# A macaron transformer layer on one core: three tables of steps written anew, two GpSimd additions held behind VectorE, whole-tile products and three more runs of filling products in the opening

## The reference

```python
def ffn(x):                      # W1: 512x128, W2: 128x512
    Wq1, Wq2 = quantize(W1), quantize(W2)   # clip(round(W / (mean|W| + 1e-5)), -1, 1)
    return relu(x @ Wq1.T + b1) @ Wq2.T + b2
def attn(x):
    q, k, v = (heads(x @ W.T + b) for W, b in ((Wq, bq), (Wk, bk), (Wv, bv)))
    q, k = rope(q, k)
    p = softmax(q @ k.T / sqrt(8))          # 16 heads, 512 x 512 each, for each of 8 sequences
    return merge(p @ v) @ Wo.T + bo
x = x + 0.5 * ffn(layernorm(x))
x = x + attn(layernorm(x))
x = x + 0.5 * ffn(layernorm(x))
```

## Time and profile before

| | |
|---|---|
| median of 3 runs | 520.1 us (518.65 to 523.45) |
| the profiled execution, its own time | 519.27 us |
| its span from the first to the last instruction | 517.5 us |
| TensorE busy / VectorE busy / ScalarE busy / GpSimd busy | 488.3 / 409.2 / 347.5 / 203.5 us |
| mean granted TensorE clock | 0.990 of full speed |
| start of the first `e` of batch 0, 1, 2, 3, 4, 5, 6, 7 | 54.67, 122.00, 180.83, 239.11, 296.37, 348.18, 400.74, 451.62 us |

### The profile page before, as it was taken

The page is one execution under the profiler, slowest core; times in us unless marked ns, Lnnn a source line. Parts: engine busy times, 40 slices in busy tenths (PEclk is TensorE's granted clock), DMA queues, the critical chain, the costliest instruction groups (busy, mean ns, idle before and its releaser), DMA issues.

```text
span 517.5 us, 13169 instructions
## 1 busy us (share of the span) xinstructions
PE 488.3 (94%) x5455; PEld 227.2 (44%) x5455; DVE 409.2 (79%) x644; ACT 347.5 (67%) x429; POOL 203.5 (39%) x226
## 2 busy tenths in 40 slices
PE   6689999899999999999999999999999999998996
PEld 3455435252354535363354533443344334443445
DVE  5776997958998689877897699779987998898124
ACT  5627565757767687577867677766776778578841
POOL 3507065707338080825534183336342650005001
PEclk8998999999999999999999999999999999999999
DMA  8047037203350136203450147024612451000000
GB/s 276 25 163 166 11 120 208 42 4 123 124 125 3 40 125 177 56 3 97 171 125 4 45 146 189 16 63 162 148 23 56 156 149 36 23 3 3 3 22 20
DMA packets 20007, 44.63 MB, mean 86 GB/s; under 512 B 2860, under 2 KB 5420, under 8 KB 18924
## 3 DMA queue, kind: packets, MB, share of 16 engines
q1 hardware_dynamic: 18636, 41.96, 28.4%
q10 hardware_dynamic: 1312, 1.84, 1.0%
HBM read 20.58 MB, written 18.87 MB: 76 GB/s over the span
## 4 chain that ended last, share of the span: by engine, by line
PE 72%; DVE 15%; ACT 6%; issue 3%; DMA 2%; POOL 1%; ACTq 0%; DVEq 0%; POOLq 0%
PE heads_acc L577 19%; PE side L584 18%; PE unit L560 14%; PE unit L541 12%; DVE maxima L906 8%; ACT probs L788 3%; ACT hidden L778 3%; PE side L621 2%; PE side L611 1%; DMA q_scratch<-q_parts 1%; PE heads_acc L652 1%; PE side L606 1%; PE unit L584 1%; DVE stats_ffn L873 1%; DMA resid<-in_x 1%
## 5 line engine op out<-in xcount | busy, mean ns | idle before, releaser
L906 DVE TENSOR_REDUCE maxima<-unit 128x2 f32<-128x1024 f32 x256 | 304.7, 1219 | 57.3 <-PE unit L541 56.4
L788 ACT ACTIVATE probs<-unit 128x1024 f32<-128x1024 f32 x256 | 256.2, 1025 | 99.1 <-PE unit L560 98.2
L577 PE MATMUL heads_acc<-probs,v_heads 128*32 128x512 f32 x1024 | 135.3, 601 | 0.6 <-ACT probs L788 0.4
L560 PE MATMUL unit<-q_stack,k_stack 64*128 64x512 f32 x512 | 118.7, 463 | 5.9 <-DVE maxima L906 5.3
L541 PE MATMUL unit<-k_stack,q_stack 62*128 62x512 f32 x512 | 114.0, 442 | 2.5 <-DVE maxima L906 1.0
L560 PEld LDWEIGHTS unit<-q_stack,k_stack 64*128 64x128 f32 x512 | 47.6, 184 | 72.6 <-DVE maxima L906 33.9
L541 PEld LDWEIGHTS unit<-k_stack,q_stack 62*128 62x128 f32 x512 | 48.3, 185 | 61.9 <-ACT probs L788 30.6
L584 PE MATMUL side<-w_q,hidden 128*32 128x128 f32 x1664 | 53.5, 275 | 0.0
L386 POOL TENSOR_TENSOR rope_a_k<-k,cos_t 128x512 f32<-128x512 f32 x7 | 8.9, 1277 | 101.6 <-ACT k L775 101.6
L584 PEld LDWEIGHTS side<-w_q,hidden 128*32 128x32 f32 x1664 | 43.2, 110 | 12.4 <-issue 8.9
L1062 POOL TENSOR_SCALAR var_eps_ffn<-mean_var_ffn 128x4 f32<-128x4 f32 x15 | 3.7, 249 | 108.1 <-DVE mean_var_ffn L877 108.1
(11 more groups left out here) (144 smaller groups left out, 461.0 us busy)
## 6 DMA issues: line engine op xcount, KB each, us to landing
k_scratch<-k_parts SPq DMA_DIRECT2D x16, 512.0 KB, 2.9
q_scratch<-q_parts SPq DMA_DIRECT2D x14, 512.0 KB, 3.3
k_stack<-k_scratch SPq DMA_DIRECT2D x16, 384.0 KB, 5.4
q_stack<-q_scratch SPq DMA_DIRECT2D x16, 384.0 KB, 6.8
resid<-in_x SPq DMA_DIRECT2D x8, 256.0 KB, 4.8
k_stack<-k_scratch SPq DMA_DIRECT2D x16, 128.0 KB, 2.5
k_swap<-k SPq DMA_DIRECT2D x14, 128.0 KB, 2.3
q_swap<-q SPq DMA_DIRECT2D x14, 128.0 KB, 2.3
```

Source lines behind the costliest of these rows:

```text
L560: mm = pe.matmul(to[:, e, :], k_stack[part, quad // NQ % 2, pair, kt * P:(kt + 1) * P], q_stack[part, quad // NQ % 2, pair, :], start=True ...
L577: mm = pe.matmul(heads_acc[32 * j:32 * j + 32, :], v_heads[:, b % 2, at, ODD * odd:ODD * odd + 32], probs[:, burst % RING, j, :], start=(k ...
L788: act.activation(probs[:, burst % RING, 2 * pp:2 * pp + 2, :], unit_of(PLACE["exp", n]), ACT.Exp, scale=SCALE).then_inc(s_exp, 1)
L906: dve.tensor_reduce(maxima[:, quad % 2, :, r], unit_of(PLACE["max", k]), AX_X, ALU.max).then_inc(s_max, 1)
```

## The change

There are four parts.

1. The strings of `FIRST`, `STEADY` and `LATER` are written anew. Each table keeps its words, so that the same pieces are done; they stand in other places. SP's stores, maxima rows and swaps at the end of a batch now follow the table's order instead of a fixed one.
2. GpSimd waits at two `add_bias`-like additions: `add_bias("ffn1", 1)` in the opening waits until VectorE has written `normed["attn"]` of batch 0, and the last `xb["ffn2"]` waits until VectorE has written all of the last `normed["ffn2"]`.
3. `column_tiles` takes the width as an argument; the steps of `PROLOGUE` use 128 (whole tiles), all others 32 as before. The four `ffn1_down` pieces of batch 2 beside the first `m` are no part of `PROLOGUE` and stay at 32.
4. `fill` runs at three more places: 14 before the wait for the thresholds of the quantisation, 14 before `ffn1_up0` of batch 1, 8 before `ffn1_up0` of batch 2. In `PROLOGUE` a fill now stands ahead of the waits for weights and constants, not behind them.

```diff
 FIRST = [
-    "e m fill1", "e m first_max_T1", "e m m fill2 attn_T@1", "e m m fill2 k@1", "e m m q@1", "e m m ffn1_T@3",
+    "e m fill1", "e first_max_T1 m", "e m m fill2 attn_T@1", "e m m k@1 fill2", "e m m", "e q@1 m m ffn1_T@3",
...
 LATER = [
-    "e m", "e pv m heads_copy1@-1", "e m heads_T1@-1", "e pv m", "e m pv max_T1", "e m out_T", "e m out", "e m pv",
-    "e ffn2_stats m", "e pv m v", "e m", "e pv max_T2 m", "e m ffn2_T", "e m pv", "e m ffn2_up0",
+    "e m", "e pv m heads_copy1@-1", "e m pv", "e max_T1 m", "e m heads_T1@-1", "e m pv", "e m out_T", "e m out", "e m pv",
+    "e ffn2_stats m", "e pv pv m", "e v m", "e m pv max_T2", "e m ffn2_T", "e m pv ffn2_up0", "e m attn_stats ffn2_up1",
...
-FILL = {("ffn1_up", 0, 0): 8, ("k_first", 0, 0): 6}
+FILL = {("ffn1_up", 0, 0): 8, ("ffn1_up", 0, 1): 14, ("ffn1_up", 0, 2): 8, ("k_first", 0, 0): 6}
+FILL_BEFORE_THR = 14
...
-                if 0 < b < B:
-                    sp.wait_ge(s_y, b)
-                    sp.dma_start(out[b - 1].rearrange("(p t) d -> p t d", t=T), batch_rows(b - 1)).then_inc(s_stored, 16)
-                if on("values", b):
-                    max_row((b + 1) * NQ)
-                if on("proj", b):
-                    swap("k", b + 2)
-                    swap("q", b + 2)
+
+                for word in " ".join(PLANS[b]).split() if b < B else ():
+                    if word == "ffn2_down3" and b > 0:
+                        sp.wait_ge(s_y, b)
+                        sp.dma_start(out[b - 1].rearrange("(p t) d -> p t d", t=T), batch_rows(b - 1)).then_inc(s_stored, 16)
+                    elif word == "max_T4" and on("values", b):
+                        max_row((b + 1) * NQ)
+                    elif word in ("k", "q") and on("proj", b):
+                        swap(word, b + 2)
...
-            def column_tiles(to, lhs, rhs, start, stop):
-
-                for c in range(0, P, TILE_COLS):
-                    mm = pe.matmul(to[c:c + TILE_COLS, :], lhs[:, c:c + TILE_COLS], rhs, start=start, stop=stop)
+            def column_tiles(width, to, lhs, rhs, start, stop):
+
+                for c in range(0, P, width):
+                    mm = pe.matmul(to[c:c + width, :], lhs[:, c:c + width], rhs, start=start, stop=stop)
                 return mm
...
+            fill(FILL_BEFORE_THR)
             pe.wait_ge(s_thr, 1)
             pe.wait_ge(s_ident, 16)
             for use in PROLOGUE:
+                fill(FILL.get(use[:3], 0))
                 if use[:3] == ("ffn1_up", 0, 0):
                     pe.wait_ge(s_wq, 1)
...
-                fill(FILL.get(use[:3], 0))
-                side_work(use)
+                side_work(use, P)
...
             ln_rstd("attn", 0)
+
+            pool.wait_ge(s_normed["attn"], T)
             add_bias("ffn1", 1)
...
             pool.wait_ge(s_y, last)
+            pool.wait_ge(s_end_normed, T)
             pool.tensor_tensor(xb["ffn2"][:], batch_rows(last), b2_half[:].to_broadcast([P, T, D]), ALU.add).then_inc(s_end_xb, 1)
```

12 lines of the change are left out of this document (5 added, 7 removed), and 28 rows, old and new, of tables (FIRST, LATER, STEADY).

## The result

The changed kernel took 522.64 us (median of 20 runs, 519.62 to 526.53), the kernel before beside it 519.31 us (median of 20, from 516.88). The ratio is 1.0045, 95% interval [1.0027, 1.0064]: slightly slower, where 513.7 us had been forecast. The profiled execution took 519.62 us, the quickest of the twenty, with a span of 517.8 us, so its trace shows the mechanism but less than the whole loss.

What follows compares the result with a forecast made beforehand. TensorE's own instruction order was taken to bound `STEADY` and `LATER`, dependent steps the opening. Gains 1.4 (GpSimd) + 1.0 (opening) + 1.4 (shape changes) + 1.0 + 0.8 (waits) = 5.6 us off 519.27 gave 513.7 us, range 508.5 to 519.5.

Steps and rivals of the forecast that it cites:

- The step that failed: Waits in the `LATER` batches: new table gains 0.2 us each of 1.0 us TensorE idle, bounds 0.5 us either way.
- The prediction's last sentence: Tables shift GpSimd's operations against VectorE's; hitting its short pieces more often would make the forecast wrong altogether; no size or chance.
- GpSimd's additions: Two new waits keep additions off VectorE's normalising pieces: 0.94 us at the end, 0.5 in the opening; sum 1.4 us.
- The start of the opening: Opening of batch 0: new fills close TensorE's gaps, clock may rise, down products start sooner; 1.0 us gained, bounds 0 and 1.3.
- Whole tiles: Opening's up and down products in 128-wide tiles: taken as zero, with 1.3 us slower and 0.2 gained as range.
- rival (d): Whole tiles' weight loads and products take turns: batch 0's down block takes 2 x 3.7 us, 517.4 us in all; chance 0.02.
- `FIRST` and `STEADY`: New tables: 77 to 72 shape changes in `FIRST`, 54 to 53 in `STEADY`, 0.12 us each; waits 1.0 us in batch 0 only.
- Rival (a): New tables: `pv` too close behind its exponentials, TensorE waits 0.4 us at 26 new places, 10 us, 524 us; chance 0.09.

Runs made afterwards that it cites:

- hold_before: Kernel before plus one wait: GpSimd holds the rotation of `q` until VectorE's first-quarter split of the maxima, from batch 1 on; 515.61 us, ratio 0.9893.
- fills_waits: Kernel before with the new fills and GpSimd's two new waits, narrow tiles and old tables; 518.45 us, ratio 0.9956.
- tiles_waits: Kernel before with whole tiles in the opening and GpSimd's two new waits, no new fills, old tables; 518.19 us, ratio 0.9968.
- open_all: Kernel before with new fills, whole tiles in the opening and GpSimd's two new waits, old tables; 515.65 us, ratio 0.9897.
- fills_only: Kernel before with the new fills and their new places alone; 520.94 us, ratio 1.0037.
- tiles_only: Kernel before with whole tiles in the opening alone; 519.54 us, ratio 1.0009.
- fills_tiles: Kernel before with the new fills and whole tiles in the opening, GpSimd not held, old tables; 517.94 us, ratio 0.9976.
- later_new: Kernel before with the new `LATER` table and the SyncE loop that follows the tables; 527.28 us, ratio 1.0133.
- later_old: Changed kernel with the `LATER` table of the kernel before; 514.78 us, ratio 0.9900.
- hold_split: later_old, with GpSimd holding the rotation of `q` until VectorE's first-quarter split of the maxima, from batch 1 on; 508.49 us, ratio 0.9799.

## Why the prediction was wrong, point by point

**The step that failed** is in the tables, under waits: "in `LATER` 1.0 us idle, of which 0.59 is one wait for VectorE, and I take 0.2 us each, 0.8 together", with "bounds 0.5 us either way each". Batches 4, 5 and 6 became 3.31, 2.48 and 2.10 us longer. The two waits at `max_T4` are 3.5 us of these 7.9, the collision at the start of batch 4, which the new `STEADY` brings, 1.4, and two half-clock stretches some 3.2 (1.58 us each, last section). The waits of the new order in batch 6 cost 1.6 more, and against them stand two collisions of the old table that are gone, 0.86 us each by hold_before. The step looked at TensorE's words and at SP's list only. It did not follow `k` and `q` into GpSimd's queue, so it never saw that the rotary steps now stood beside VectorE's split of the maxima. The prediction's last sentence named this ("hit its short pieces more often than now") without a price or a chance, which put it at nothing in the sum. The rows for it were there: two uncontested pieces of under 0.2 us, pieces of 1.15 us beside GpSimd in the trace of before, and the order of GpSimd in the changed kernel. A rival with two collisions in each of two batches, 1.0 us each, and one half-clock stretch of 1.6 us behind them would have given 513.7 + 4.0 + 1.6 = 519.3 us, an estimate made afterwards.

**GpSimd's additions**: right. 0.94 us was priced for the end, 0.98 measured; pieces of 1.2 us forecast for `normed_attn`, 1.12 measured. In the opening, where 0.5 us was priced, the first `m` comes 0.5 to 0.7 us sooner with the waits than without (fills_waits, tiles_waits and open_all against fills_only, tiles_only and fills_tiles).

**The start of the opening**: right in mechanism (the clock stays at 1.00), too small in size. The fourteen fills ran at full clock and did not hold the transposes up (0.45 us had been taken), the input landed 0.46 us sooner, which is chance, and from the first up product to the down block it took the 3.2 us forecast at full clock: 2.04 us, where 1.3 was the upper bound. With the wait's 0.5 us, 1.5 us were forecast; the first `e` came 2.84 us sooner with the three edits of the opening and 3.64 us sooner with the tables too.

**Whole tiles**: right. 3.64 us for a down block in 32 records; rival (d) (7.4 us) did not come. An up product takes 0.22 us and not the 0.46 of the upper bound.

**`FIRST` and `STEADY`**: 0.6 us for changes of shape and 1.0 for waits were forecast in batch 0; it stayed at 67.3 to 67.4 us in every trace without a half-clock stretch there, whatever the table. This term failed too. `STEADY` was forecast at 0.12 us a batch and gave 1.48, 1.16 and 0.15. It gave them in TensorE's busy time, not in its waits: in batch 2 this fell from 58.03 us to 56.08, while the idle time rose from 0.25 to 1.04. One change of shape less cannot be that at 0.12 us each; which words do it is open. (The old table's batch 2 itself takes 57.50 us in later_new, busy 57.27, so some 0.8 us of the 1.16 is spread.)

**Rival (a)**, a `pv` too close behind its exponentials, was the one case given for slower than before, and it did not happen. The page's group of the `pv` products in the changed kernel, with no idle time before them over all 1024:

```profile
L579 PE MATMUL heads_acc<-probs,v_heads 128*32 128x512 f32 x1024 | 134.5, 605 | 0.0
```

The forecast for everything but `LATER` was 4.3 us; later_old gained 5.6 us. That these are so near is in part luck: by the lengths of its trace the opening gave 3.7 us for 1.5, `FIRST` nothing for 1.6, `STEADY` 2.8 for 0.4, and the start of batch 4 took 1.4 for which there was no term. What turned a gain into a loss is in one table.

## What to carry to other kernels

A step that is moved must be followed onto every engine that it feeds: here six strings on TensorE moved two GpSimd instructions of 1.3 us onto two VectorE instructions of 0.17 us that TensorE was waiting for. List the shortest SBUF instructions on the critical path and see which long GpSimd instruction stands beside each; where one does, a wait that holds GpSimd until the short one is done cost nothing here, where GpSimd is busy 39% of the span, and was worth about 1% (hold_before, and hold_split against later_old). A wait put down to a long instruction (`maxima`) may be owed to a short one ahead of it in the same queue.
